# Ternary weights rounded in one VectorE pass with a sign on ScalarE, a new order of the front, and weighted sums without a zero product

## The reference

```python
def _weight_quant(w):
    scale = 1.0 / jnp.clip(jnp.mean(jnp.abs(w)), 1e-05)
    wq = jnp.clip(jnp.round(w * scale), -1.0, 1.0) / scale
    return w + jax.lax.stop_gradient(wq - w)
...
    scores = jnp.where(mask == 0, jnp.float32(NEG), scores)
    weights = jax.nn.softmax(scores, axis=-1)
    out = jnp.einsum('bhqk,bhkd->bhqd', weights, v)
...
    gate = jax.nn.silu(_bitlinear(x, w_gate))
    up = _bitlinear(x, w_up)
    return _bitlinear(gate * up, w_down)
x = x + jnp.tanh(g_xattn[0]) * _L0_xattn_ref(_layernorm(x, axis=-1), ctx_1024, ctx_1024, mask_Bx1x1xS2_ik0, ...)
x = x + jnp.tanh(g_ffn[0]) * _L0_ffn_ref(_layernorm(x, axis=-1), L0_ffn_w_gate, L0_ffn_w_up, L0_ffn_w_down)
```

## Time and profile before

| | |
|---|---|
| median of 3 runs | 1356.69 us |
| profiled execution's own time | 1358.6 us |
| its span | 1356.8 us |
| mean granted TensorE clock | 0.977 |
| PE busy | 1260.9 us (93%) |
| DVE busy | 1144.6 us (84%) |
| ACT busy | 878.1 us (65%) |
| POOL busy | 735.1 us (54%) |

### The profile page before, as it was taken

One profiled execution on the slowest core, in us unless ns is written; L12 is line 12 of the kernel. 1 busy time (PEld: TensorE's weight loads), 2 busy tenths in 40 slices (PEclk: granted clock), 3 DMA queues, 4 the chain that ended last, 5 costly groups with the idle time before them and its releaser, 6 DMA issues.

```text
span 1356.8 us, 26014 instructions
## 1 busy us (share of the span) xinstructions
PE 1260.9 (93%) x7424; PEld 630.1 (46%) x7998; DVE 1144.6 (84%) x2631; ACT 878.1 (65%) x1350; POOL 735.1 (54%) x1187
## 2 busy tenths in 40 slices
PE   4776799999999999999999999999999999999996
PEld 2223444545454454545454454545445454544542
DVE  6877597898979798897979799797979989797884
ACT  5886747557584756758575665758475675847663
POOL 2113645546574664657465564756456465746662
PEclk8978899999999999999999999999999999999998
DMA  9785346574653647364564646455464736445333
GB/s 341 223 247 112 75 104 140 110 163 107 148 135 105 138 102 186 97 156 110 131 148 94 161 108 153 107 140 132 105 152 108 180 94 150 121 113 116 90 79 73
DMA packets 386793, 181.64 MB, mean 134 GB/s; under 512 B 324323, under 2 KB 357987, under 8 KB 385123
## 3 DMA queue, kind: packets, MB, share of 16 engines
q1 hardware_dynamic: 386736, 181.04, 55.1%
HBM read 61.32 MB, written 35.46 MB: 71 GB/s over the span
## 4 chain that ended last, share of the span: by engine, by line
PE 58%; DVE 29%; issue 5%; DMA 3%; ACT 3%; POOL 1%; SPq 1%; POOLq 0%; ACTq 0%; DVEq 0%
PE bank L1244 21%; PE bank L1256 15%; PE bank L1185 5%; DVE region L1046 5%; PE bank L1105 4%; DVE nmax L985 4%; PE bank L1106 3%; PE bank L1107 3%; DVE xh L975 3%; DVE xbig L1013 2%; DVE hmx L1052 2%; DVE st L1017 2%; DVE xn L970 2%; PE bank L1207 1%; PE bank L1209 1%
## 5 line engine op out<-in xcount | busy, mean ns | idle before, releaser
L628 POOL TENSOR_TENSOR region<-region,up 128x512 f32<-128x512 f32 x256 | 344.7, 1350 | 140.5 <-DVE region L1046 80.0
L1244 PE MATMUL bank<-tern_gate,region 128*128 128x512 fp8e4 x1024 | 264.8, 381 | 8.4 <-DMA region<-zb 7.3
L1244 PE MATMUL bank<-tern_up,region 128*128 128x512 fp8e4 x1024 | 263.8, 380 | 0.2 <-ACT up L781 0.2
L1256 PE MATMUL bank<-tern_down,region 128*128 128x512 fp8e4 x1024 | 234.0, 382 | 10.1 <-DMA region<-hb 9.4
L773 ACT ACTIVATE region<-bank,fs 128x512 f32<-128x512 f32 x256 | 177.4, 697 | 83.5 <-PE bank L1244 83.1
L1046 DVE SCALAR_TENSOR_TENSOR region<-region,bank 128x512 f32<-128x512 f32 x256 | 173.4, 682 | 59.9 <-ACT region L773 54.7
L1052 DVE TENSOR_REDUCE hmx<-region 128x1 f32<-128x512 f32 x256 | 170.7, 678 | 56.3 <-POOL region L628 56.2
L619 POOL TENSOR_TENSOR work<-work 124x512 f16<-124x512 f32 x160 | 191.7, 1220 | 28.7 <-ACT work L742 28.5
L582 POOL TENSOR_TENSOR rs<-mv,lnc 128x1 f32<-128x1 f32 (+1 forms) x80 | 26.7, 334 | 290.8 <-DVE mv L1020 274.0
L781 ACT ACTIVATE up<-bank 128x512 f32<-128x512 f32 x256 | 152.7, 612 | 19.6 <-PE bank L1244 18.8
L786 ACT ACTIVATE hb<-region 128x2048 bf16<-128x2048 f32 x64 | 122.7, 1918 | 56.0 <-DVE region L1068 56.0
(11 more groups left out here) (144 smaller groups left out, 2393.7 us busy)
## 6 DMA issues: line engine op xcount, KB each, us to landing
q_stack<-q_rows SPq DMA_DIRECT2D x96, 256.0 KB, 5.1
xbig<-in_x SPq DMA_DIRECT2D x16, 1024.0 KB, 5.4
q_rows<-q SPq DMA_DIRECT2D x64, 256.0 KB, 2.0
out_y<-o SPq DMA_DIRECT2D x64, 256.0 KB, 3.3
q_stack<-mT SPq DMA_DIRECT2D x32, 256.0 KB, 3.7
region<-in_wgT SPq DMA_DIRECT2D x4, 1024.0 KB, 8.3
region<-in_wuT SPq DMA_DIRECT2D x4, 1024.0 KB, 7.2
region<-in_wdT SPq DMA_DIRECT2D x4, 1024.0 KB, 5.9
```

The lines of the kernel that those rows point to most:

```text
L628: nc.gpsimd.tensor_tensor(ht, ht, up[:, n % 2, :], ALU.mult).then_inc(hmul_ready, 1)
L1244: ins = T.matmul(pb[2 * (n % 2) + w][:, :], xqT[:, k, tok], tern[w][:, k * FF + n * GT:k * FF + (n + 1) * GT], start=(k == 0), stop=(k == ...
L1256: ins = T.matmul(pb[2][:, :], hT[:, t % 2, k, :], tern[2][:, k * GT:(k + 1) * GT], start=(k == 0), stop=(k == FK - 1))
```

## The change

It does four things. Every quarter is scaled and rounded in one VectorE pass (`wr`), which writes `region` in place as before; ScalarE then takes the sign of the value minus MAGIC (its bias is a column of `con`, set by a memset of its own), which is -1, 0 or 1. The two clipping pieces and ScalarE's rounding piece are gone, and two semaphores with them. The front's strings are written anew. In the weighted sums the zero product is left out together with its operand `v_none` and a memset on GpSimd; the chunks run in the order 0, 2, 4, 1, 3, the first product of chunk 0 has the start flag, and the first product of chunks 1 and 3 is split in two, so that its middle head, written for the first time, is apart from the outer two, which accumulate. `_ORDER` and `_LAST` strings stay.

```diff
+CHUNKS = [c for c in range(0, CH, 2)] + [c for c in range(1, CH, 2)]
...
 SYNC_FIRST = """
-    W:lx00 W:lc00 W:lk00 W:lz00 W:lw00 W:w00 M:tx00 W:w01 W:w02 W:w03 W:lv00 M:tx10 W:lx10 W:lw10 M:tx20 M:tx30
+    W:lx00 W:lk00 W:lc00 W:lw00 W:lz00 W:w00 W:w01 M:tx00 W:w02 W:w03 W:lv00 M:tx10 M:tx20 W:lx10 W:lw10 W:w10
...
-            def weight_round(_, i, j):
-
-                act.wait_ge(wmean_ready, i + 1)
-                nc.scalar.activation(region[:, j * FF:(j + 1) * FF], region[:, j * FF:(j + 1) * FF], ACT.Copy, bias=MAGIC,
-                                     saturate=False, scale=c(R_G + i)).then_inc(wround_ready, 1)
-
             def weight_ternary(_, i, j):
 
-                act.wait_ge(wclip_ready, 4 * i + j + 1)
-                nc.scalar.activation(tern[i][:, j * FF:(j + 1) * FF], region[:, j * FF:(j + 1) * FF], ACT.Copy, bias=-MAGIC,
+                act.wait_ge(wround_ready, 4 * i + j + 1)
+                nc.scalar.activation(tern[i][:, j * FF:(j + 1) * FF], region[:, j * FF:(j + 1) * FF], ACT.Sign, bias=c(MINUS_MAGIC),
                                      saturate=False).then_inc(tern_ready, 1)
...
             def clear_scalars(*_):
-                V.memset(con[:, 2:], 0.0).then_inc(con_cleared, 1)
+                V.memset(c(MINUS_MAGIC), -MAGIC)
+                V.memset(con[:, 2:MINUS_MAGIC], 0.0).then_inc(con_cleared, 1)
...
-            def weight_upper(_, i, j):
+            def weight_round(_, i, j):
 
                 dve.wait_ge(wmean_ready, i + 1)
-                V.tensor_scalar(region[:, j * FF:(j + 1) * FF], region[:, j * FF:(j + 1) * FF], c(R_G + i), 1.0,
-                                ALU.mult, ALU.min).then_inc(wupper_ready, 1)
-
-            def weight_lower(_, i, j):
-
-                if j % 2:
-                    dve.wait_ge(wround_ready, 2 * i + j // 2 + 1)
-                    V.tensor_scalar(region[:, j * FF:(j + 1) * FF], region[:, j * FF:(j + 1) * FF], MAGIC - 1.0, MAGIC + 1.0,
-                                    ALU.max, ALU.min).then_inc(wclip_ready, 1)
-                    return
-                dve.wait_ge(wupper_ready, 2 * i + j // 2 + 1)
-                V.tensor_scalar(region[:, j * FF:(j + 1) * FF], region[:, j * FF:(j + 1) * FF], -1.0, MAGIC,
-                                ALU.max, ALU.add).then_inc(wclip_ready, 1)
+                V.tensor_scalar(region[:, j * FF:(j + 1) * FF], region[:, j * FF:(j + 1) * FF], c(R_G + i), MAGIC,
+                                ALU.mult, ALU.add).then_inc(wround_ready, 1)
...
-                for cc in range(CH):
+                for cc in CHUNKS:
...
-                    if cc == 0:
-                        T.matmul(bank[:, heads * HW:HH * HW], hi, v_none[:, :], start=True, stop=False)
-                    T.matmul(dst, hi, both[:, :, 0:HW], start=False, stop=False)
+                    if cc % 2 == 0:
+                        T.matmul(dst, hi, both[:, :, 0:HW], start=(cc == 0), stop=False)
+                    else:
+                        T.matmul(dst[:, 1, :], hi, both[:, 1, 0:HW], start=False, stop=False)
+                        T.matmul(dst[:, 0::2, :], hi, both[:, 0::2, 0:HW], start=False, stop=False)
                     T.matmul(dst[:, :, 0:DH], hi, both[:, :, HW:VW], start=False, stop=False)
-                    ins = T.matmul(dst, lo, both[:, :, 0:HW], start=False, stop=(cc == CH - 1))
+                    ins = T.matmul(dst, lo, both[:, :, 0:HW], start=False, stop=(cc == CHUNKS[-1]))
```

More of the change, by code:

```diff
@@ L98 @@
+    Q:mT00
 """
 SCALAR_FIRST = """
[L100 to L104 removed]
@@ L105 @@
-    A:zb10 A:zq20 A:zb20 A:zq30 A:zb30
+    M:xh00 M:xh10 W:tn00 W:oh00 W:ws00 M:xh20 W:ws01 W:ws02 W:ws03 W:wh00 M:xh30 W:wt00 W:kh00 W:wt01 W:wt02
+    W:wt03 W:ws10 W:vw00 W:ws11 R:q00 R:q10 W:ws12 W:ws13 R:q20 W:wh10 N:xh00 R:q30 N:xh10 W:wt10 W:vh00 W:wt11
+    N:xh20 N:xh30 W:wt12 W:ws20 W:wt13 W:ws21 R:mT00 W:ws22 Q:q00 Q:q10 W:ws23 Q:q20 A:sc00 A:sc01 Q:q30 A:sc02
+    A:sc03 A:sc04 A:sc10 A:sc11 A:sc12 A:ah00 A:sc13 A:ah01 A:sc14 A:ah02 W:wt20 A:ah03 A:ah10 W:wt21 A:ah11
+    A:ah12 A:ah13 W:wt22 W:wt23 A:zq00 Q:mT00 A:zb00 A:zq10 A:zb10 A:zq20 A:zb20 A:zq30 A:zb30
@@ L113 @@
[L113 to L115 removed]
+    W:hc00 M:ln00 M:xn00 M:xl00 M:xn10 M:xn20 W:wx00 M:xl10 W:hd00 M:xn30 W:wp00 M:xl20 W:km00 W:wm00 W:wr00
+    W:kp00 W:wr01 M:xl30 W:wr02 W:kc00 W:wr03 W:wl00 N:ln00 W:wx10 W:vm00 N:xn00 W:wp10 R:q00 R:q10 N:xn10
+    W:vp00 W:wm10 R:q20 W:wr10 R:q30 N:xl00 R:s00 N:xl10 W:wr11 R:s01 W:wr12 R:s10 N:xn20 N:xn30 R:s11 N:xl20
@@ L116 @@
+    R:s20 N:xl30 R:s21 R:s30 W:wr13 W:wl10 R:s31 R:mh00 W:vc00 W:ys00 Q:q00 Q:q10 W:es00 W:wm20 Q:q20 Q:q30
+    W:wr20 Q:s00 Q:s01 Q:s10 Q:s11 Q:s20 A:pv00 A:al00 A:pv01 A:pv02 Q:s21 A:al01 A:pv03 A:al02 W:wr21 A:pv10
+    A:al03 A:pv11 A:al10 W:wr22 A:pv12 A:al11 W:wr23 A:pv13 A:al12 Q:s30 A:al13 A:wo00 A:st00 Q:s31 A:wo10
+    A:st10 Q:mh00 A:zn00 A:wo20 A:st20 A:za00 A:wo30 A:zn10 A:st30 A:za10 A:zn20 A:za20 A:zn30 A:za30
 """
@@ L212, in gated_cross_attention_and_ternary_ffn @@
         v = sb("v", [CR, 2, V_AT[CH]], f16)
-        v_none = sb("v_none", [CR, (HH - len(SPANS[0])) * HW], f16)
         tern = [sb(n, [P, 4 * FF], f8) for n in ("tern_gate", "tern_up", "tern_down")]
@@ L286, in gated_cross_attention_and_ternary_ffn @@
         tern_in = [sem(f"tern_in{j}") for j in range(4)]
-        wsum_quarter, wmean_ready, wupper_ready, wround_ready = (
-            sem(n) for n in ("wsum_quarter", "wmean_ready", "wupper_ready", "wround_ready"))
-        wsum_ready, wsum_all, wclip_ready, tern_ready, gate_tanh, cast_ready, con_cleared = (
-            sem(n) for n in ("wsum_ready", "wsum_all", "wclip_ready", "tern_ready", "gate_tanh", "cast_ready", "con_cleared"))
+        wsum_quarter, wmean_ready, wround_ready = (
+            sem(n) for n in ("wsum_quarter", "wmean_ready", "wround_ready"))
+        wsum_ready, wsum_all, tern_ready, gate_tanh, cast_ready, con_cleared = (
+            sem(n) for n in ("wsum_ready", "wsum_all", "tern_ready", "gate_tanh", "cast_ready", "con_cleared"))
         ln1_stats, ln1_rstd, xn_ready, xh_ready, xl_ready = (
@@ L312, in gated_cross_attention_and_ternary_ffn @@
          CG0, KAP0, OUT0, ACC) = range(26)
+        MINUS_MAGIC = 38
         def c(i, n=1, rows=P):
@@ L556, in _ @@
             nc.gpsimd.memset(v[:, :, :], 0.0).then_inc(cast_ready, 1)
-            nc.gpsimd.memset(v_none[:, :], 0.0).then_inc(cast_ready, 1)
             nc.gpsimd.memset(mhl[:, :, :], 0.0).then_inc(cast_ready, 1)
```

38 lines of the change are left out of this document (12 added, 26 removed).

## The result

The changed kernel is slower: 1380.42 us median (1376.74 to 1384.71, four runs) against 1356.37 us (1352.64 to 1358.62, four runs), a ratio of 1.0182 with a 95% interval of 1.0152 to 1.0212. The forecast was 1349.5 us, with a range of 1343 to 1356; 1380.42 lies far outside.

The account below looks back on a forecast made before the run. TensorE and VectorE were taken to share the bound, with order and latency bounding the front. Steady part -5.2 and front -2.0 us, together -7.2, off the median 1356.7 gave 1349.5 us, range 1343 to 1356.

Parts of the forecast that it names:

- Steady part: -5.2 us: Weighted sums in groups 1 to 15: each step on TensorE's chain saves 50 ns; range -7.8 to -1 us.
- a shift of TensorE by 0.35 us a turn passes through: At the first `down`'s output: VectorE, idle 0.46 us there, doesn't hold back seven steps' saving; 0.1 us to spare.
- That goes: Weighted-sum step: the zero product's 198 columns, 86 ns, are removed from TensorE's chain.
- Front: -2.0 us: Path to the first gate product: 0 up to group 1's queries, then -1.3 and -0.7 us; range -7.0 to +4.8.
- The 1.3 us for the transpose ahead of `mT`: End of the front, SyncE's queue: `zb`'s first transpose leaves ahead of two `mT` transfers, gaining 1.3 us.
- The passes: Ternary weights in the front: VectorE's 12 passes 15.4 us in all (-7.0), ScalarE's signs 1.99 us each (-10.8).
- VectorE becomes the bound of the steady part: Rival, steady turns: VectorE follows too closely, only a third of the 5.2 us is gained; 1354.5 us, chance 0.13.
- the transpose queue of the front: Rival, front: group 1's first `xT` waits behind a late up-weight quarter, 10.0 us later; 1359.5 us, chance 0.05.
- short products that don't pipeline: Rival, weighted sums: 33 columns can't cover a weight load, each step 86 ns slower; 1363.1 us, chance 0.02.

Follow-up runs that it names:

- e14: The kernel before with GpSimd's wait, the swap in GpSimd's order and the new weighted sums alone, tiles in place: 1342.74 us, ratio 0.9888 to the kernel before.
- e4: The kernel before with the new weighted sums alone, the place of `v_none` kept as a spare tile: 1367.41 us, ratio 1.0082 to the kernel before.
- e1: The changed kernel with an unused tile of `v_none`'s size in its place, so later tiles regain their old addresses: 1372.49 us, ratio 1.0124 to before.
- e5: e1 plus a wait: GpSimd's last product of a group's third tile follows VectorE's quantising pass of the second: 1360.18 us, ratio 0.9953 to before.
- e9: e5 plus a swap in GpSimd's order, the third tile's third product ahead of a second-layernorm step: 1345.95 us, ratio 0.9914 to before.
- e13: e9 with 15 instead of 17 products a weighted-sum step, leaving out part of the values' precision: 1344.47 us, ratio 0.9910 to before.
- e11: The kernel before, all tiles in place, with GpSimd's added wait of e5 alone: 1355.70 us, ratio 0.9989 to the kernel before.
- e15: e12 with the new front and ternary code alone, zero product kept and tiles in place: 1346.40 us, ratio 0.9912 to the kernel before.
- e12: The kernel before with GpSimd's wait and the swap of e9, none of the change's parts: 1343.06 us, ratio 0.9896 to the kernel before.

## Why the prediction was wrong

**"Steady part: -5.2 us".** The price was right: a step takes 0.58 us, of the 0.58 to 0.59 named, and 33 columns take 0.03 us from start to start, within 18 to 32 ns. The Trainium skill's 25 ns (TensorE: Matmul & The Clock Gate, Wait — 56ns, not 53.3ns?) are compatible with it. Its 81 ns for a pair of load and product (the same page, Back-to-back issue gap) are given for 128 columns and don't carry over to the 33 to 99 columns here: 17 pairs in 0.58 us are 34 ns each. The failed step is the one after: that a shift of TensorE by 0.35 us a turn passes through, checked at one place only, behind `down`. There the idle time, forecast to shrink from 0.46 to 0.1 us, was 0.86 us (ahead of the output that begins at 650.44) in the change, and still 0.30 in e14, where only the sums are new; so that place was never the tight one. Two other places were closer. At the first, GpSimd and VectorE changed places and a turn got 0.9 to 1.0 us longer (e4, e1, e5). At the second, `silu` behind ScalarE's `hb`, a part of the rest is lost (e9, e13). With the race repaired the sums give 0.09 (e5 against e11) to 0.19 us a turn.

**"That goes" of `v_none`.** I counted its product and its memset and not its place in memory. It was the only part of the change that reached the transposes of the steady turns, and it cost 0.6 to 0.7 us a turn, about 8 us in all by e1. Nothing in the rows of before could show this price, but that an allocation moves all those behind it was in the diff.

**"Front: -2.0 us".** In the change's profiled execution it came out: 2.4 us at the first gate product, and 2.0 at the mark (191.80 against 193.84). That was luck: this execution has the highest clock of all 18 profiles from 82 to 140 us (0.91; the others have 0.79 to 0.85). Over executions it didn't come out: by the medians above, the mark is 1.7 us later with the new front, in ranges that overlap almost wholly. The 1.3 us for the transpose ahead of `mT` was counted for the first tile, while in e15 the ones behind `mT` pay. The passes cost what I took: 1.278 us on VectorE, 1.99 on ScalarE.

**The rivals.** *VectorE becomes the bound of the steady part* was nearest. Its size was what happened once the two causes were away: 0.13 us a turn instead of 0.35 (e9 against e12), though what then held TensorE was a VectorE step that waited for ScalarE. It had no room for a turn that gets longer. The two slower rivals, the transpose queue of the front and short products that don't pipeline, didn't occur: group 1's queries began at 82.41 against 82.15. *A wait that takes the place of the one removed* was looked for in orders and queues, where two engines that exclude each other don't show: the pass's length in the profile of before looked like its cost, and the 3.73 us of two 1.27 us products, which was the sign, was never read.

## What to carry to other kernels

Print the addresses of all tiles when one is added or dropped, and if the landings of DMA transposes grow with it, try multiples of 256 bytes for their sources and targets. In a kernel whose engines run in a fixed order, look in the trace for instructions of VectorE and GpSimd that last longer than their like; where two that exclude each other become ready within a tenth of a microsecond, an explicit wait that fixes their order was worth more here than the saved product (1.04 against 0.19 us a turn). Follow a saving on the busiest engine past every place where it hands over, not only the tightest one seen.
